# A six-stage decoder kernel: loading the first cross-attention unit inside the stage before, moving the query projections, and splitting the normed rows up front

## The chip, the core and the metric

The kernel runs on one core of a Trainium2 chip. TensorE (PE) multiplies matrices, VectorE (DVE), ScalarE (ACT) and GpSimd (POOL) do the elementwise work, SyncE (SP) issues most of the DMAs. The engines run their own instruction queues and meet at semaphores. The metric is the device time of one execution in microseconds (us), as the median of several runs.

## The reference

Two decoder layers over x, 4 sequences (b) of 256 tokens by 256 features; each sublayer is added to the residual. In sequence:

```
x = x + slot_attention(layernorm(x))            # layer 0, 16 heads, 64 slots a head
x = x + cross_attention(layernorm(x), ctx)      # layer 0, ctx: 4 x 1601 rows of 256
x = x + mixture_of_experts(layernorm(x))
x = x + differential_attention(layernorm(x))    # layer 1
x = x + masked_cross_attention(layernorm(x), ctx)
x = x + ternary_ffn(layernorm(x))

# the cross attention (16 heads of 16), the part that the change touches
q = rms_norm(x @ q_w + q_b) * norm_q_w
k = rms_norm(ctx_txt @ k_w + k_b) * norm_k_w;   v = ctx_txt @ v_w + v_b     # 1344 keys
ki = rms_norm(ctx_img @ k_img_w + ...) ;        vi = ctx_img @ v_img_w + ...  # 257 keys
out = (softmax(q k / 4) v + softmax(q ki / 4) vi) @ o_w + o_b
```

## The kernel before

Each sublayer is a stage with a list of steps. A step is a tuple such as ("q", 3), and each engine's program walks the same list in the same order and emits its own part of each step (SP the DMAs). Between two stages all five engines drain and meet (`boundary`). What runs on an engine is therefore ordered by the list alone, and every engine is in order.

The slot attention ("gsa") goes through 16 units (4 head groups x 4 sequences), unit m of which is spread over passes m to m+3. Before the first pass, `norm_steps(0, 0)` normalises and transposes the first sequence's 256 rows, and then the other six 128-row tiles follow. `h_split` b cuts the turned rows `hT` of sequence b into a high and a low part (`h_parts`): a cast on ACT (L748), a subtraction on POOL (L920). TensorE's products of queries and keys (`qk`, L1755 to L1757) read both parts of the sequence. In the kernel before, the split of sequence m+1 stands in pass m, woven between that pass's other steps.

Passes 12 to 18 also carry steps of the cross attention ("xa", `xa_early`): its weights, the key and value projections of sequence 0, its keys normed, turned, split into three bf16 parts (`xa_keys`) and stored to DRAM (`k_store`, L1109), and the queries of sequences 0 to 2. `queries(b)` is the set of six steps for one sequence: two tiles projected (L1464) and biased (L1560), one norm (`q_norm`, a chain of small DVE operations), two tiles turned (L1469) and split (L1362, L1367, L1369, L1374), one store to DRAM (L1105).

The cross attention stage has 16 units, 4 heads of one sequence each, of 13 key tiles ("steps" below: step m is the m-th key tile, unit n begins at step 13n). For unit n, `load` fetches keys and queries from DRAM into one of four buffers `kst`/`qst`: six key DMAs (L1100), six query DMAs (L1090), and for the first four loads one of constant rows (L987). `max` (32 matmuls L1137, each reduced on DVE, L1250) finds the largest score of each query; the negated maxima are turned and written into `qst` by six small DMAs (`neg_turn`, L1121). Then `exp` (L1156, ACT L1211) and `pv` (L1177) run over the 13 tiles. Meanwhile `projections(b)` and `xa_keys(b)` make the next sequence's keys in the steps 1 to 21 after the sequence before began. `xa_steps` gives each step a number and sorts by it: loads 0 to 3 stand ahead of everything, `queries(3)` at 4 to 10, the step `later` (weights for what follows, and about 3 MB copied into `moe_places_h`, L1679 and L1682) at 13, `max` of unit n from 13n-18.2 to 13n-5.2, `neg_turn` at 13n-3.2. A rotating set of three PSUM banks serves max, q, q_turn, kv and k_turn alike.

## Time and profile before

| what | value |
| --- | --- |
| median of 3 runs | 2068.56 us (2068.51 to 2073.98) |
| the profiled execution: its own time, its span | 2059.21 us, 2057.4 us |
| granted TensorE clock, mean over the span | 0.925 of full |
| PE, DVE busy, share of the span | 86%, 66% |
| ACT, POOL busy | 41%, 23% |
| slot attention stage, about | 0 to 653 us |
| cross attention stage, about | 653 to 1190 us |

Busy shares are averages over six stages with different limits, so they bound nothing by themselves. The table of windows gives for any stretch the busy time of each engine, the granted clock, and the share of the DMA engines that was busy. The timeline gives single instructions; the brackets at a row's end give the engine's idle time before it and what ended it.

### The profile page before, as it was taken

How to read it: one execution, taken by the hardware profiler on the slowest of the kernel's cores; microseconds unless marked ns; L12 is line 12 of the kernel's file. 1: busy time of each engine (PE TensorE's matmuls, PEld its weight loads, DVE VectorE, ACT ScalarE, POOL GpSimd, SP SyncE). 2: the span in 40 equal slices, each digit the busy share in tenths (PEclk: the TensorE clock that was granted, in tenths of full speed). 3: DMA queues.
4: the chain of work that ended last, by engine and by line, in shares of the span. 5: the costliest groups of instructions: out<-in, count | busy, mean ns of one | idle time of the engine just before them, and what ended most of it. 6: DMA issues, size and time to landing. Idle time of an engine off the chain costs nothing.

```text
span 2057.4 us, 32234 instructions
## 1 busy us (share of the span) xinstructions
PE 1769.9 (86%) x12150; PEld 1108.5 (54%) x12150; DVE 1348.0 (66%) x3123; ACT 838.1 (41%) x1339; POOL 465.6 (23%) x694
## 2 busy tenths in 40 slices
PE   4899999998963788989989979995887698999978
PEld 4788888888652233434434445663454244444446
DVE  6676676766575677687778543445455787888843
ACT  2333333333331145456455722441232165656651
POOL 4443444444122011020010021442000013211100
PEclk9999999999986699999999979998898699999988
DMA  3000010010014548228163064545320156655000
GB/s 113 5 27 11 21 32 11 24 61 1 16 40 113 94 93 144 32 91 101 34 118 45 2 229 162 203 167 114 73 61 20 39 73 127 76 89 80 7 1 21
DMA packets 91396, 142.65 MB, mean 69 GB/s; under 512 B 14549, under 2 KB 59737, under 8 KB 91242
## 3 DMA queue, kind: packets, MB, share of 16 engines
q1 hardware_dynamic: 78978, 118.87, 27.7%
q10 hardware_dynamic: 10392, 16.58, 2.8%
q0 software_dynamic: 1872, 5.13, 0.7%
q8 instruction: 98, 1.61, 0.3%
q14 instruction: 56, 0.46, 0.1%
HBM read 109.62 MB, written 32.03 MB: 69 GB/s over the span
## 4 chain that ended last, share of the span: by engine, by line
PE 63%; DVE 20%; issue 6%; ACT 4%; DMA 4%; SPq 2%; POOL 2%; ACTq 0%; POOLq 0%; DVEq 0%
PE bank L1177 8%; PE bank L1137 8%; PE bank L1156 7%; PE bank L1859 5%; PE bank L1478 4%; PE bank L1755 3%; PE bank L729 3%; PE bank L1878 3%; PE bank L1757 3%; PE bank L1756 3%; DVE xa_part_max L1250 2%; PE bank L2267 2%; SPq L1121 1%; DMA xa_qst<-xa_q_parts 1%; PE bank L2252 1%
## 5 line engine op out<-in xcount | busy, mean ns | idle before, releaser
L1250 DVE TENSOR_REDUCE xa_part_max<-bank 128x1 f32<-128x448 f32 (+1 forms) x512 | 273.5, 569 | 67.5 <-PE bank L1137 62.4
L1211 ACT ACTIVATE xa_e<-bank 128x1024 f32<-128x1024 f32 (+1 forms) x208 | 212.7, 1023 | 137.9 <-PE bank L1156 136.0
L1211 ACT ACTIVATE ca_e<-bank 128x1024 f32<-128x1024 f32 (+2 forms) x208 | 196.6, 957 | 99.3 <-PE bank L1156 91.9
L1250 DVE TENSOR_REDUCE ca_part_max<-bank 128x1 f32<-128x400 f32 (+1 forms) x384 | 205.8, 570 | 35.3 <-PE bank L1137 31.5
L1137 PE MATMUL bank<-xa_kst,xa_qst 122*128 122x448 bf16 (+1 forms) x512 | 171.4, 360 | 41.6 <-DMA xa_qst<-xa_q_parts 20.0
L1137 PE MATMUL bank<-ca_kst,ca_qst 125*128 125x400 bf16 (+2 forms) x512 | 160.8, 350 | 24.3 <-DMA ca_qst<-ca_q_parts 11.8
L1156 PE MATMUL bank<-xa_qst,xa_kst 128*128 128x256 bf16 (+1 forms) x832 | 128.6, 277 | 19.5 <-DMA xa_qst<-xa_negT 19.5
L1177 PE MATMUL bank<-xa_e,xa_vaug 128*17 128x256 f32 (+2 forms) x1792 | 140.7, 389 | 1.0 <-ACT xa_e L1211 0.6
L1177 PE MATMUL bank<-ca_e,ca_vaug 128*17 128x256 f32 (+2 forms) x1664 | 125.8, 375 | 7.9 <-ACT ca_e L1211 7.0
L1137 PEld LDWEIGHTS bank<-xa_kst,xa_qst 122*128 122x128 bf16 x512 | 48.7, 98 | 151.9 <-DVE xa_part_max L1250 85.0
L1156 PE MATMUL bank<-ca_qst,ca_kst 128*128 128x256 bf16 (+2 forms) x832 | 121.6, 269 | 0.3 <-ACT ca_e L1211 0.2
L933 POOL TENSOR_TENSOR gsa_qk<-gsa_qk,gsa_rot 128x512 f32<-128x512 f32 x64 | 81.9, 1280 | 169.5 <-DVE gsa_rot L849 169.5
L1137 PEld LDWEIGHTS bank<-ca_kst,ca_qst 125*128 125x128 bf16 x512 | 47.5, 98 | 121.7 <-DVE ca_part_max L1250 56.9
L1156 PEld LDWEIGHTS bank<-xa_qst,xa_kst 128*128 128x128 bf16 (+1 forms) x832 | 81.2, 100 | 54.3 <-DMA xa_qst<-xa_negT 22.9
L1478 PE MATMUL bank<-xa_wkv,shared 128*128 128x512 f32 (+2 forms) x224 | 108.3, 609 | 0.4
L1156 PEld LDWEIGHTS bank<-ca_qst,ca_kst 128*128 128x128 bf16 (+1 forms) x832 | 79.7, 101 | 27.3 <-issue 6.8
L1859 PE MATMUL bank<-moe_gu,moe_rowsT 128*128 x184 | 86.5, 593 | 0.1
L2373 DVE TENSOR_REDUCE da_neg<-bank 128x2 f32<-128x512 f32 x64 | 41.3, 687 | 51.8 <-PE bank L2267 51.8
L1322 POOL TENSOR_SCALAR_AFFINE_SELECT ca_e<-ca_e 128x248 f32<-128x248 f32 (+2 forms) x48 | 23.7, 507 | 223.2 <-ACT ca_e L1211 223.2
L847 DVE TENSOR_TENSOR gsa_qk<-bank,gsa_cos 128x512 f32<-128x512 f32 x64 | 43.6, 682 | 45.7 <-PE bank L1757 45.4
L1247 DVE CUSTOM_DVE_ANT_0 ca_masked_scores<-bank,ca_pen 128x272 f32<-128x272 f32 (+1 forms) x128 | 64.5, 504 | 10.9 <-PE bank L1137 10.0
L344 PE MATMUL bank<-ident,h 128*128 128x128 f32 x48 | 18.7, 390 | 58.6 <-DVE h L333 58.1
(373 smaller groups left out, 3994.6 us busy)
## 6 DMA issues: line engine op xcount, KB each, us to landing
xa_kst<-xa_k_parts SPq DMA_DIRECT2D x96, 200.1 KB, 8.7
ca_kst<-ca_k_parts SPq DMA_DIRECT2D x96, 200.1 KB, 7.4
xa_k_parts<-xa_parts SPq DMA_DIRECT2D x8, 1200.8 KB, 6.5
ca_k_parts<-moe_ctx_parts SPq DMA_DIRECT2D x8, 1200.8 KB, 5.7
moe_gu<-in_expert_gate_up SPq DMA_DIRECT2D x8, 1024.0 KB, 15.3
shared<-in_ctxT_split ACTq DMA_DIRECT2D x4, 1601.0 KB, 6.6
moe_ctxT<-in_ctxT SPq DMA_DIRECT2D x8, 800.5 KB, 8.1
ca_cv<-in_ctx ACTq DMA_DIRECT2D x4, 1536.0 KB
```

Source lines behind the costliest of these rows:

```text
L729: m = e.matmul(ps[:, 0:D], ogT[i][:, h_, :], wo[g % 2][:, h_, :], start=(h_ == 0), stop=(h_ == G4 - 1))
L933: e.tensor_tensor(qb[:], qb[:], rb[:], ALU.add).then_inc(*qk_ready(n))
L1137: e.matmul(work[:, 0:hi - lo], qb[0:self.AUG, h_, i * P:(i + 1) * P], kb[0:self.AUG, h_, lo:hi], start=True, stop=True).then_inc(*mx_mm(t, ...
L1156: mm = e.matmul(o, kb[:, j, k0:k0 + rows], qb[:, j, first:T], start=True, stop=True)
L1177: mm = e.matmul(bank[4][32 * j:32 * j + VW, s * T + lo:(s + 1) * T], vb[r0:r1, v, g * UNIT + j, :], self.e[m % 3][r0:r1, j, lo:T], start=f ...
L1211: e.activation(self.e[m % 3][0:rows, :, first:T], banks[m % 2][0:rows].rearrange("p a (h t) -> p (a h) t", t=T)[:, :, first:T], ACT.Exp, s ...
L1247: e.tensor_tensor_reduce(self.masked_scores[:, 0:hi - lo], work[:, 0:hi - lo], self.pen[:, i, 0:hi - lo], 1.0, FAR, ALU.add, ALU.max, top) ...
L1250: e.tensor_reduce(top, work[:, 0:hi - lo], AX.X, ALU.max).then_inc(*reduced(t, *step))
L1478: m = e.matmul(ps[r0:r1, :], xctx[:, c, k0 + r0:k0 + r1], wkv[s][:, c, :], start=(c == 0), stop=(c == DC - 1))
L1755: e.matmul(ps, l[:, 0], r[:, 0], start=(n == 0), stop=False)
L1756: e.matmul(ps, l[:, 0], r[:, 1], start=False, stop=False)
L1859: m = e.matmul(bank[j], l, r, start=(c == 0), stop=(c == DC - 1))
```

## The change

Five things. `h_split` of sequences 1 to 3 leaves the passes: each sequence is split as soon as its two tiles are turned, before the first pass (`normed_rows`). `queries(1)` and `queries(2)` leave the last pass of the slot attention. `load 0` joins pass 17, behind the store of the keys of sequence 0; for that its query buffer `qst0` is allocated among the early tiles, and SP waits for the slot attention's last `a` and `v` products first. In the cross attention `queries(b)` for b = 1, 2, 3 now stand at 10.5 to 21 steps after sequence b-1 began, beside `xa_keys(b)`. Loads 1, 2 and 3 stand at -99, 2 and 15 instead of ahead of everything.

```diff
@@ gsa_steps
+            def normed_rows(b):
+                for i in range(b * TB, (b + 1) * TB):
+                    yield "norm", 0, i
+                    yield "norm_turn", 0, i
+                yield "h_split", b
...
@@ ahead(m)
-                if m + 1 < B:
-                    yield "h_split", m + 1
@@ xa_early(m)
                     yield from xa_keys(0)
-                if m == GSA_UNITS + 2:
-                    yield from queries(1)
-                    yield from queries(2)
+                    yield "load", 0
@@ before the passes
-            for b in range(1, B):
-                for i in range(b * TB, (b + 1) * TB):
-                    yield "norm", 0, i
-                    yield "norm_turn", 0, i
+            yield from normed_rows(1)
+            yield from normed_rows(2)
+            yield from normed_rows(3)
@@ Attention
-                self.qst = [sb(f"qst{i}", [P, UNIT, T], BF16) for i in range(AHEAD)]
+                self.qst = [*qst, *(sb(f"qst{i}", [P, UNIT, T], BF16) for i in range(len(qst), AHEAD))]
@@ xa_steps
-            parts = [list(XA.flow()), spread(queries(B - 1), 4, 10), [(whole_unit, ("later", 0))]]
+            parts = [list(XA.flow()), *(spread(queries(b), (b - 1) * UNITS * whole_unit + 10.5, (b - 1) * UNITS * whole_unit + 21) for b in range(1, B)), [(whole_unit, ("later", 0))]]
...
-                if n % UNITS or not n:
-                    parts.append([(start - 3 * whole_unit + 1 if n >= AHEAD else n - 100, ("load", n))])
+                if n % UNITS:
+                    parts.append([(start - 3 * whole_unit + 1 if n >= AHEAD else -99 if n == 1 else start - 2 * whole_unit + 2, ("load", n))])
@@ xa_sp_step
+            elif kind == "load":
+                if n == 0:
+                    q.wait_ge(a_mm, G4 * GSA_UNITS - 1)
+                    q.wait_ge(v_mm, GSA_UNITS - 1, TB - 1)
+                if n < AHEAD:
+                    XA.stacks.constants_rows(q, n)
+                XA.load_sp(q, n)
```

SP at the end of the slot attention, in the kernel before: the store of the keys of sequence 0, two query stores (six DMAs), and after the boundary load 0, load 1 and the start of load 2.

```order
L1109 DMA xa_k_parts<-xa_parts 128x3x1601 x2
L1105 DMA xa_q_parts<-xa_q_split 128x2x256 x6
L987 DMA xa_kst<-in_consts 32x4x1601
L1100 DMA xa_kst<-xa_k_parts 16x4x1601 x6
L1090 DMA xa_qst0<-xa_q_parts 16x4x256 x6
L987 DMA xa_kst<-in_consts 32x4x1601
L1100 DMA xa_kst<-xa_k_parts 16x4x1601 x6
L1090 DMA xa_qst1<-xa_q_parts 16x4x256 x6
L987 DMA xa_kst<-in_consts 32x4x1601
```

The same place in the changed kernel (its line numbers are 1 to 9 higher).

```order
L1110 DMA xa_k_parts<-xa_parts 128x3x1601 x2
L988 DMA xa_kst<-in_consts 32x4x1601
L1101 DMA xa_kst<-xa_k_parts 16x4x1601 x6
L1091 DMA xa_qst0<-xa_q_parts 16x4x256 x6
L988 DMA xa_kst<-in_consts 32x4x1601
L1101 DMA xa_kst<-xa_k_parts 16x4x1601 x6
L1091 DMA xa_qst1<-xa_q_parts 16x4x256 x6
L1122 DMA xa_qst0<-xa_negT0 1x4x256 x6
L988 DMA xa_kst<-in_consts 32x4x1601
```

The two query stores have left this place, load 0 follows the key store directly, and the six small DMAs of unit 0's maxima come ahead of load 2; the boundary now stands between load 0 and load 1.

Further on in SP's queue, the kernel before: the end of load 3, the maxima of units 0 and 1 with the query store of sequence 3 between them, then the rows of `later`.

```order
L987 DMA xa_kst<-in_consts 32x4x1601
L1100 DMA xa_kst<-xa_k_parts 16x4x1601 x6
L1090 DMA xa_qst3<-xa_q_parts 16x4x256 x6
L1121 DMA xa_qst0<-xa_negT0 1x4x256 x6
L1105 DMA xa_q_parts<-xa_q_split 128x2x256 x3
L1121 DMA xa_qst1<-xa_negT1 1x4x256 x6
L1676 DMA xa_wo<-in_xa_o_w 128x2x256
```

The changed kernel, from the maxima of unit 1 to load 3.

```order
L1122 DMA xa_qst1<-xa_negT1 1x4x256 x6
L1685 DMA xa_wo<-in_xa_o_w 128x2x256
L1686 DMA xa_bo<-in_xa_o_b 128x256
L1687 DMA moe_wgate<-in_gate_w 128x2x8
L1688 DMA moe_places_h<-in_unsent 2944x2
L1691 DMA moe_places_h<-in_x 1024x256 x2
L1691 DMA moe_places_h<-in_x 896x256
L988 DMA xa_kst<-in_consts 32x4x1601
L1101 DMA xa_kst<-xa_k_parts 16x4x1601 x6
L1091 DMA xa_qst3<-xa_q_parts 16x4x256 x6
```

Load 3 has moved from the head of the stage to behind the copies into `moe_places_h`.

POOL at the start of the slot attention, before: splits of sequence 0 and of two weights, then the rotated queries and keys (`gsa_qk`), with the split of sequence 1 behind the fourth of them.

```order
L920 TENSOR_TENSOR gsa_h_parts<-hT,gsa_h_parts 128x2x256
L925 TENSOR_TENSOR gsa_wq<-gsa_w,gsa_wq 128x1024
L925 TENSOR_TENSOR gsa_wk<-gsa_w,gsa_wk 128x1024
L933 TENSOR_TENSOR gsa_qk<-gsa_qk,gsa_rot 128x512 x3
L906 AFFINE_SELECT gsa_aT<-gsa_aT 128x2x128
L933 TENSOR_TENSOR gsa_qk<-gsa_qk,gsa_rot 128x512
L920 TENSOR_TENSOR gsa_h_parts<-hT,gsa_h_parts 128x2x256
```

The same place in the changed kernel.

```order
L921 TENSOR_TENSOR gsa_h_parts<-hT,gsa_h_parts 128x2x256
L926 TENSOR_TENSOR gsa_wq<-gsa_w,gsa_wq 128x1024
L926 TENSOR_TENSOR gsa_wk<-gsa_w,gsa_wk 128x1024
L921 TENSOR_TENSOR gsa_h_parts<-hT,gsa_h_parts 128x2x256 x3
L934 TENSOR_TENSOR gsa_qk<-gsa_qk,gsa_rot 128x512 x3
L907 AFFINE_SELECT gsa_aT<-gsa_aT 128x2x128
L934 TENSOR_TENSOR gsa_qk<-gsa_qk,gsa_rot 128x512
```

The splits of sequences 1 to 3 stand ahead of the first `gsa_qk`.

## Rows read from the trace of the kernel before

**Rows 1.** Windows: us, engines busy (instructions), PE clock, DMA share, GB/s.
```profile
652.90:667.70 14.80, 0.00 (x0) 0.01 (x1) 2.42 (x5) 0.00 (x0) 3.04 (x1) 0.50 1.03 179
667.70:690.50 22.80, 20.51 (x47) 4.68 (x47) 22.02 (x47) 0.36 (x1) 0.84 (x4) 0.50 1.07 174
699.50:751.00 51.50, 47.99 (x222) 20.20 (x223) 30.92 (x88) 19.17 (x44) 2.13 (x6) 0.93 0.10 33
```

**Rows 2.** Timeline, 640 to 700 us: start, length, engine, line, operation, [idle before].
```profile
667.72 16.71 PE L1137 MATMUL bank<-xa_kst,xa_qst 122*128 122x448 bf16 x35 [17.97 <-DMA xa_qst<-xa_q_parts]
699.49 0.82 PE L1156 MATMUL bank<-xa_qst,xa_kst 128*128 128x256 bf16 x3 [9.56 <-DMA xa_qst<-xa_negT]
```

**Rows 3.** Timeline of the slot attention's last pass.
```profile
627.89 2.04 POOL L949 TENSOR_TENSOR gsa_og<-gsa_og,gsa_rr 128x512 f32<-128x512 f32 x2 [2.52 <-DVE gsa_rr L889]
633.25 1.06 PE L721 MATMUL bank<-ident,gsa_og 128*128 128x128 f32 x4
...
640.44 0.74 DVE L322 BATCH_NORM_STATS2 stats<-x 128x6 f32<-128x256 f32 x2
644.10 0.40 DVE L333 TENSOR_SCALAR h<-x,mv,rstd 128x256 f32<-128x256 f32 x1
650.77 0.67 POOL L1374 TENSOR_TENSOR xa_q_split<-xa_r,xa_q_split 128x256 bf16<-128x256 f32 x1 [0.23 <-DVE xa_q_split L1369]
```

**Rows 4.** Timeline of SP's DMA issues, 594 to 700 us.
```profile
625.40 1.63 SPq L1109 DMA_DIRECT2D xa_k_parts<-xa_parts  x2
...
653.12 0.35 SPq L987 DMA_DIRECT2D xa_kst<-in_consts  x1
...
686.71 3.79 SPq L1121 DMA_DIRECT2D xa_qst<-xa_negT  x6
```

**Rows 5.** Landing times of the key store issued at 625.40.
```profile
DMA to landing us min/median/max: 5.0/6.4/7.7
```

**Rows 6.** Timeline: unit 3's maxima, SP's issue and the matmul that waited.
```profile
808.79 3.66 SPq L1121 DMA_DIRECT2D xa_qst<-xa_negT  x6
...
814.39 0.61 PE L1156 MATMUL bank<-xa_qst,xa_kst 128*128 128x256 bf16 x4 [0.76 <-DMA xa_qst<-xa_negT]
```

**Rows 7.** Waits of PE, 22 to 150 us, and timeline around the first.
```profile
PE bank L1755 <- POOL gsa_h_parts L920: 9.6, 2, 5.6
...
42.23 0.55 PE L1755 MATMUL bank<-gsa_h_parts,gsa_wq 128*128 128x256 f32 x1 [5.65 <-POOL gsa_h_parts L920]
...
34.21 3.36 DVE L837 RECIPROCAL gsa_enz<-bank 128x512 f32<-128x512 f32 x1
...
34.88 0.63 ACT L748 CAST gsa_h_parts<-hT 128x512 fp32r<-128x512 f32 x1
```

**Rows 8.** One query set: windows of tiles xa_qq and xa_q_split, then timeline.
```profile
715.00:748.00 33.00, 0.82 (x4) 0.45 (x4) 1.73 (x4) 1.02 (x4) 1.00 0.07 17
...
715.00:748.00 33.00, 1.44 (x4) 0.73 (x2) 1.34 (x2) 1.00 0.07 17
...
717.27 1.03 PE L1464 MATMUL bank<-xa_wq,hT 128*128 128x256 f32 x4
...
729.60 0.16 DVE L1563 TENSOR_SCALAR xa_q_sv<-xa_q_ss 128x2 f32<-128x2 f32 x1
...
731.96 0.88 DVE L1568 SCALAR_TENSOR_TENSOR xa_qq<-xa_qq,xa_q_sr,xa_nq 128x256 f32<-128x256 f32 x2
```

**Rows 9.** Windows while the keys of sequences 1 and 2 are turned.
```profile
751.00:791.00 40.00, 32.57 (x267) 14.17 (x265) 35.04 (x82) 20.66 (x30) 9.84 (x18) 0.98 0.72 159
883.00:912.00 29.00, 23.47 (x188) 10.49 (x185) 27.00 (x65) 15.26 (x25) 8.31 (x13) 1.00 0.03 11
```

**Rows 10.** SP's copy in `later`, a window behind it, unit 3's first maximum on PE.
```profile
753.30 8.66 SPq L1682 DMA_DIRECT2D moe_places_h<-in_x  x3
...
775.00:780.00 5.00, 3.90 (x33) 1.72 (x32) 4.69 (x13) 2.72 (x5) 2.05 (x4) 1.00 0.01 2
...
779.85 0.36 PE L1137 MATMUL bank<-xa_kst,xa_qst 122*128 122x448 bf16 x1
```

More of the change, by code:

```diff
@@ L362, in build @@
         XA_TILES = TXT // P + 1 + 2
-        XA_EARLY = ("q", "q_norm", "q_turn", "q_store", "fetch", "kv", "k_norm", "k_scale", "k_turn", "k_store", "xa_w", "xa_const")
+        XA_EARLY = ("q", "q_norm", "q_turn", "q_store", "fetch", "kv", "k_norm", "k_scale", "k_turn", "k_store", "xa_w", "xa_const", "load")
         q_mm, q_biased, q_squared, q_scaled, q_ss_taken = local("gsa", "xa_q_mm"), local("gsa", "xa_q_biased"), local("gsa", "xa_q_squared"), local("gsa", "xa_q_scaled"), local("gsa", "xa_q_ss_taken")
@@ L992, in build, with __init__ @@
         class Attention:
-            def __init__(self, ctx, tag, keys, scale, tiles, chunks, sets, masked=False, k_dram=None, q_dram=None, stacks=None, vaug=(), parts=None):
+            def __init__(self, ctx, tag, keys, scale, tiles, chunks, sets, masked=False, k_dram=None, q_dram=None, stacks=None, vaug=(), parts=None, qst=()):
                 self.tag, self.keys, self.scale, self.tiles, self.chunks = tag, keys, scale, tiles, chunks
@@ L1406, in build @@
         qq, q_parts = sb("qq", [P, TB, D]), sb("q_split", [P, 3, DC, T], BF16)
-        XA = Attention(xa_ctx, "xa", CTX, HD ** -0.5, xa_tiles, [(0, third), (third, 2 * third), (2 * third, TXT), (TXT, CTX)], 2, vaug=(xa_vaug0,), parts=xa_parts)
+        xa_qst0 = sb("qst0", [P, UNIT, T], BF16)
+        XA = Attention(xa_ctx, "xa", CTX, HD ** -0.5, xa_tiles, [(0, third), (third, 2 * third), (2 * third, TXT), (TXT, CTX)], 2, vaug=(xa_vaug0,), parts=xa_parts, qst=(xa_qst0,))
         XA.x_stage = 2
@@ L1683, in xa_sp @@
                 else:
-                    if step[0] == "load" and step[1] < AHEAD:
-                        XA.stacks.constants_rows(q, step[1])
                     XA.sp(q, step)
```

## The prediction

> **What bounds the kernel now.** I read the page's busy shares first: TensorE leads with 86% of the span, so what it stands idle for is what there is to gain. The table of windows shows the largest hole, between the first two stages. From 652.9 to 667.7 us no TensorE work runs at all while the DMA engines are full (share 1.03); for 22.8 us more DVE is saturated (22.02 busy) by unit 0's maxima, with TensorE at half clock (0.50); only at 699.49 does the first score matmul start [rows 1, 2]. The timeline says what ended each wait: unit 0's query and key rows from DRAM at 667.72, and its six rows of maxima at 699.49, after 9.56 us in which TensorE had nothing [rows 2]. The first unit then is bound by TensorE, 47.99 of 51.5 us [rows 1]. Two other places matter: the start, where TensorE waits 9.6 us in two waits for POOL's split of a later sequence [rows 7], and the stretches in which keys are turned and split, where DVE is busy 35.04 of 40 and 27.00 of 29 us [rows 9].
>
> **The splits up front.** The first wait lasts 5.65 us, up to 42.23, so TensorE was free at 36.58 [rows 7]. What is late next is its PSUM bank, held until DVE's reciprocal ends at 34.21 + 3.36 = 37.57: 4.66 us can go. Of the second wait (9.6 - 5.6 = 4.0 us) I know no next bound, so 0 to 4.0 goes. Against it: each split's cast costs ACT 0.63 us between the copies that free the transposes' banks [rows 7], three of them 1.9 us, partly covered by DVE's norm of the next tile; I take 0.5. POOL's three subtractions fall where it has no queued work yet. Bounds: -8.7 + 0.5 at best, nothing gained (+1.9) at worst, if later passes were waiting for something else anyway. I take -6, near the two waits, since TensorE is the busy engine of the rest of that stage.
>
> **The hand-over.** Three things are in line: when load 0 lands, when unit 0's maxima are ready, when their six rows land.
> Load 0. It can go once the key store of sequence 0 is in DRAM: issued from 625.40, landing up to 7.7 us after [rows 4, 5], so about 633.1. Before, from the first issue at 653.12 to the first max at 667.72 it took 14.6 us [rows 2, 4]. The same 14.6 from 633.1 gives 647.7; the constant rows (of 1.8 MB a load, 0.4) go out while SP waits for the key store, which saves up to 0.7 of it. I take 647.0.
> Is the stage over by then? Before, POOL had both scaled tiles by 627.89 + 2.04 = 629.93, but TensorE's second turn of them started at 633.25, since a query turn in front of it waited for its norm chain: 3.3 us lost [rows 3]. Then came the output products, one more tile projection, the norm from its statistics at 640.44 to the first row tile at 644.10, and the last query split, which ran to 651.44 [rows 3]. Without the queries the statistics start 3.3 us and one 1.03 us projection earlier, at about 636, the first row tile is there 3.7 us later at 639.7, transposes and copies take some 2 us by my estimate from such tiles, so the boundary is at about 641.5 and, with DVE's memsets (2.42 us [rows 1]), a first max possible at 644. Load 0 at 647.0 is the later one. Gain so far 667.72 - 647.0 = 20.7.
> The maxima themselves stay 32 matmuls and reductions at DVE's pace; nothing changes there.
> The six small DMAs were issued from 686.71 to 690.50 and the matmul started at 699.49, 9.0 us after the last, behind loads 1 to 3 (the four loads went out from 653.1 with the DMA engines full, and these rows behind them landed at 699.5: some 44 us of transfers, 11 a load). Where the queue was less full, the same six ended at 812.45 and the matmul ran at 814.39: 1.9 us [rows 6]. In the change only load 1 is ahead of them; it goes out from 641.5 and both loads together need 22 us from 633, so the queue is empty by about 656, and the small DMAs go out at about 666. Gain 7.0. Together 27.7: the first score matmul at 671.8 on before's time axis. Bounds: 20.7 - 3 + 0 if load 0 shares its engines with load 1 and the small DMAs stay slow, 23.7 + 7.0 if the boundary alone decides.
> Load 2 is due at step 7.8, some 30 us after that, and goes out at once: hidden.
>
> **The query sets in the cross attention.** One set costs DVE 1.73 us on `xa_qq`, 1.44 on its split and 731.96 - 729.60 = 2.36 for the norm chain: 5.5 us. It costs TensorE 0.82 for turns and 2 x 1.03 for projections: 2.9 us [rows 8]. Before, one set (sequence 3) lay in unit 0, where TensorE bounds: -2.9. Now three sets lie where keys are turned, and there DVE is 88 and 93% busy [rows 9]: 3 x 5.5 = +16.5. Lower bound: TensorE's share alone or DVE's leftover idle, about 2.5 a set, +7.6. Upper bound: a set's length when nothing hides it, from the 640.44 that its last projection just preceded to the last split at 651.44 [rows 3], 11.0 a set, +33.0. I take DVE's busy time, because the rows show DVE as the engine without slack there.
>
> **Load 3 behind `later`.** The 3 MB copy of `later` went out from 753.30, and the DMA engines were idle again (share 0.01) from 775 [rows 10]: about 22 us of transfers. Unit 3's first max was at 779.85 [rows 10]. All of this moves up by 27.7 + 2.9 = 30.6, the max only by 25.1 (a query set now lies before it): due at 754.8. The copies end at 744.4 and load 3's 11 us end at 755.4, 757 with landing. TensorE would stand some 2 us: +2 (0 to 8).
> The Trainium skill (DMA: Bandwidth & Descriptors, Queues, rings and completion order) says that each DMA engine consumes descriptors in ring order, which speaks against this place for the load. By that rule the +2 stands, since load 3 cannot overtake the copies; if the engines took turns between them instead, load 3 would land before it is due and the sum would be 2 us better. No row of before has a load behind these copies.
>
> **Sum.** -6 - 27.7 - 2.9 + 16.5 + 2 = -18.1 us. The profiled execution took 2059.21, so it would take 2041.1. The timed runs have a median 9.35 higher; the saving lies in waits and counts the same there: 2068.56 - 18.1 = 2050.5. I count 0.3%, 6.2 us, as the least that a measurement tells from no change.
>
> **Rivals.**
> A, no change: each set costs its unhidden 11.0 us, since TensorE, in order and with three banks for everything, stops at the turn until the norm chain is through. For it: exactly this happened at 633.25 [rows 3]. Against: in the stage's steps the turns are spaced some 1.75 steps apart, with scores and maxima between. Sum: -6 - 27.7 - 2.9 + 33.0 + 2 = -1.6, 2067.0. 10%.
> B, slower: the clock does not come back. After the hand-over TensorE starts unit 0 from half clock (0.50) and got 0.93 over the 51.5 us [rows 1]. Should it stay at 1.2 GHz through the unit, its 47.99 us would be 47.99 x 0.93 / 0.50 = 89, +41 us, and the result 2050.5 + 41 = 2091.5. It decides from the point where the lost 18.1 is made up: 44.6 us of full-speed work in 44.6 / (48 + 18.1), a granted clock under 0.68 in that unit. Against: a longer hole before ended with the full clock. 4%. The Trainium skill (TensorE: Matmul & The Clock Gate, Seeing it yourself) notes a clock seen stuck low for 50 us and more; this case's trace shows no such thing in busy work after the hand-over.
> C, the early load does not do what it says: it still competes with load 1 or waits at its semaphores, and only the shorter tail counts. The first max is then 14.6 us behind the boundary of 641.5, at 656.1: gain 11.6 in place of 20.7, sum -9.0, 2059.6. For it: in before's full queue a load took the full 14.6. Against: 8 us lie between the key store's landing and the boundary. 9%.
> D, the sets are nearly free: 7.6 in place of 16.5, because reductions slide into the units behind, where DVE has room. Sum -27.0, 2041.6. 14%.
> The forecast, 2050.5, own range 2043 to 2058: 63%.
>
> **Range and chances.** 2039 to 2066 reaches from a little below D to just short of A and holds C; outside are A, B and a start and hand-over both at their best. Faster by over 0.3% (below 2062.4): 62 of the forecast's 63, 13 of D, 6 of C, 0.81. Within 0.3%: 1 + 3 + 6 of A, 1 of D, 0.11. Slower: B, 4 of A, 0.08.
>
> **What the profile after would show.** The first max of unit 0 at about 641 and its first score matmul at about 666 on the new axis (647.0 and 671.8, 6 us earlier from the start); the idle time before that matmul under 4 us, not 9.56. The two POOL waits at the start gone. No query rows between the slot attention's last output products and the boundary. The windows in which keys are turned 4 to 7 us longer each, with DVE above 90%. A wait of a few us for DMA at unit 3's first max. Wrong if the first max comes later than 650, if a key window grows by more than 9 us, or if TensorE waits over 8 us at load 3.

## The result and the profile after

| kernel | median, us | runs, us |
| --- | --- | --- |
| before | 2068.53 | 4 runs, 2064.72 to 2073.98 |
| changed | 2046.15 | 4 runs, 2042.23 to 2050.22 |

The ratio is 0.989, with a 95% interval of 0.9856 to 0.9924: the change saves 22 us, more than the 6.2 that a measurement can tell. The profiled execution took 2042.23 us (before 2059.21). Its page begins so:

```profile
span 2040.4 us, 32227 instructions
...
PE 1770.0 (87%) x12150; PEld 1102.9 (54%) x12150; DVE 1350.8 (66%) x3123; ACT 837.3 (41%) x1339; POOL 464.0 (23%) x694
```

The shares have hardly moved, so the saving must be looked for in places. First the hand-over. The timeline of PE in the changed kernel, the same two matmuls as in [rows 2], and the first maximum of unit 3 as third:

```profile
632.03 16.72 PE L1138 MATMUL bank<-xa_kst,xa_qst 122*128 122x448 bf16 x35 [5.93 <-DMA xa_qst<-xa_q_parts]
656.33 1.04 PE L1157 MATMUL bank<-xa_qst,xa_kst 128*128 128x256 bf16 x4 [2.08 <-DMA xa_qst<-xa_negT]
739.67 0.35 PE L1138 MATMUL bank<-xa_kst,xa_qst 122*128 122x448 bf16 x1 [0.24 <-DMA xa_qst<-xa_q_parts]
```

The waits of 17.97 and 9.56 us are now 5.93 and 2.08. SP's issues say why (start, length, line):

```profile
609.12 0.89 SPq L1110 DMA_DIRECT2D xa_k_parts<-xa_parts  x2
610.11 1.01 SPq L988 DMA_DIRECT2D xa_kst<-in_consts  x1
617.74 2.72 SPq L1101 DMA_DIRECT2D xa_kst<-xa_k_parts  x6
620.51 2.77 SPq L1091 DMA_DIRECT2D xa_qst<-xa_q_parts  x6
626.57 0.32 SPq L988 DMA_DIRECT2D xa_kst<-in_consts  x1
...
651.03 4.20 SPq L1122 DMA_DIRECT2D xa_qst<-xa_negT  x6
...
704.64 8.36 SPq L1691 DMA_DIRECT2D moe_places_h<-in_x  x3
713.04 4.31 SPq L988 DMA_DIRECT2D xa_kst<-in_consts  x1
```

SP issues the keys of load 0 at 617.74, 8.6 us after the key store (609.12), when the store has landed; its landing times, which answer to [rows 5]:

```profile
DMA to landing us min/median/max: 4.6/6.4/8.2
```

The last query row of load 0 lands at 631.84 and TensorE takes it at 632.03: 14.3 us from the issue of its keys, against 14.6 from its first issue before. The six small rows (651.03 to 655.23) have only load 1, issued from 626.57 and landed by 644.59, ahead of them, and the matmul starts 1.1 us behind the last; before it was 9.0 us. The end of the slot attention, which answers to [rows 3]:

```profile
613.43 2.17 PE L722 MATMUL bank<-ident,gsa_og 128*128 128x128 f32 x8 [5.88 <-POOL gsa_og L950]
...
621.43 0.74 DVE L322 BATCH_NORM_STATS2 stats<-x 128x6 f32<-128x256 f32 x2
624.87 0.74 DVE L333 TENSOR_SCALAR h<-x,mv,rstd 128x256 f32<-128x256 f32 x2
```

TensorE's eight turns of the scaled tiles follow POOL in one run, no query work comes behind, and the boundary is at 626.6.

Windows answering to [rows 1]: the empty stretch, the maxima, and the first unit from its first score matmul:

```profile
626.60:632.00 5.40, 0.00 (x0) 0.00 (x0) 2.42 (x5) 0.00 (x0) 3.04 (x1) 0.50 1.09 164
632.00:651.00 19.00, 17.39 (x40) 4.04 (x40) 18.30 (x39) 0.36 (x1) 0.84 (x4) 0.50 0.58 69
656.30:707.80 51.50, 49.43 (x243) 21.07 (x244) 29.24 (x75) 19.25 (x42) 0.83 (x4) 0.93 0.39 77
```

5.4 us are left of the 14.8 without TensorE. Unit 0 had the same granted clock as before, 0.93.

At the start, the waits of PE from 22 to 150 us, which had 9.6 us for POOL's splits [rows 7]:

```profile
PE bank L641 <- ACT gsa_es L759: 2.2, 3, 1.6
PE bank L714 <- POOL gsa_w2T L907: 1.9, 1, 1.9
PE bank L1762 <- DVE gsa_rot L850: 1.8, 2, 1.3
...
PE bank L1762 <- DVE gsa_enz L838: 1.0, 1, 1.0
```

TensorE's waits for POOL's splits are gone (the columns are us in total, times, longest). In the stretches in which the keys of the next sequence are made, I take the same 8, 16 and 16 steps of both kernels, from the start of one exponential on ACT (L1211, L1212 after) to that of another: steps 12 to 20, 60 to 76, 112 to 128. Before:

```profile
754.57:779.09 24.52, 19.14 (x147) 8.78 (x146) 23.28 (x58) 12.87 (x22) 7.64 (x12) 1.00 0.80 126
875.16:917.68 42.52, 35.09 (x283) 15.75 (x281) 39.07 (x99) 23.16 (x38) 10.68 (x22) 1.00 0.20 73
1006.95:1049.77 42.82, 35.08 (x283) 15.73 (x281) 39.09 (x99) 23.16 (x38) 10.69 (x22) 1.00 0.20 72
```

After:

```profile
707.51:738.64 31.13, 22.71 (x155) 10.74 (x153) 28.49 (x77) 14.00 (x26) 8.93 (x14) 0.89 1.05 167
836.78:886.80 50.02, 39.29 (x295) 18.58 (x293) 44.46 (x119) 24.79 (x44) 11.97 (x24) 0.93 0.20 71
974.83:1024.92 50.09, 39.53 (x295) 18.39 (x293) 44.49 (x119) 24.74 (x44) 11.98 (x24) 0.93 0.20 72
```

They grew by 6.6, 7.5 and 7.3 us, while DVE's busy time grew by 5.2, 5.4 and 5.4. The granted clock, 1.00 before, fell in each of them, and TensorE has three waits of one kind in the stage, 11.1 us together, that took 1.0 us before, this one in the first window:

```profile
719.19 1.12 PE L1186 MATMUL bank<-ident,xa_accs 128*128 128x128 f32 x4 [3.70 <-DVE xa_part_max L1251]
```

### The profile page after: what moved, and what is told of

It reads as the page before. It is cut to its first block, busy times and chain, and to the rows that moved or that the text cites. A ratio compares the mean times of both kernels' runs of the same rounds, so it can differ in the third digit from the quotient of the medians.

```text
span 2040.4 us, 32227 instructions
## 1 busy us (share of the span) xinstructions
PE 1770.0 (87%) x12150; PEld 1102.9 (54%) x12150; DVE 1350.8 (66%) x3123; ACT 837.3 (41%) x1339; POOL 464.0 (23%) x694
## 4 chain that ended last, share of the span: by engine, by line
PE 62%; DVE 20%; issue 5%; DMA 4%; ACT 4%; SPq 2%; POOL 1%; ACTq 0%; another core or an unknown queue 0%; POOLq 0%; DVEq 0%
PE bank L1178 8%; PE bank L1138 8%; PE bank L1157 7%; PE bank L1866 5%; PE bank L1480 5%; PE bank L1762 3%; PE bank L730 3%; PE bank L1885 3%; PE bank L1764 2%; PE bank L1763 2%; DVE xa_part_max L1251 2%; PE bank L2274 2%; DMA xa_qst<-xa_q_parts 2%; PE bank L2259 1%; DMA xa_k_parts<-xa_parts 1%
## 5 line engine op out<-in xcount | busy, mean ns | idle before, releaser
L1212 ACT ACTIVATE xa_e<-bank 128x1024 f32<-128x1024 f32 (+1 forms) x208 | 212.4, 1021 | 119.7 <-PE bank L1157 118.0
L1212 ACT ACTIVATE ca_e<-bank 128x1024 f32<-128x1024 f32 (+2 forms) x208 | 196.4, 956 | 101.9 <-PE bank L1157 93.9
L1157 PEld LDWEIGHTS bank<-xa_qst,xa_kst 128*128 128x128 bf16 (+1 forms) x832 | 81.7, 101 | 47.4 <-DMA xa_qst<-xa_negT 14.3
L1157 PEld LDWEIGHTS bank<-ca_qst,ca_kst 128*128 128x128 bf16 (+1 forms) x832 | 80.0, 102 | 27.8 <-issue 7.3
L1248 DVE CUSTOM_DVE_ANT_0 ca_masked_scores<-bank,ca_pen 128x272 f32<-128x272 f32 (+1 forms) x128 | 64.6, 504 | 11.7 <-PE bank L1138 11.0
L1178 PEld LDWEIGHTS bank<-xa_e,xa_vaug 128*17 128x17 f32 (+2 forms) x1792 | 29.7, 95 | 73.0 <-issue 56.1
```

The source lines that it names most:

```text
L1157: mm = e.matmul(o, kb[:, j, k0:k0 + rows], qb[:, j, first:T], start=True, stop=True)
L1178: mm = e.matmul(bank[4][32 * j:32 * j + VW, s * T + lo:(s + 1) * T], vb[r0:r1, v, g * UNIT + j, :], self.e[m % 3][r0:r1, j, lo:T], start=f ...
L1212: e.activation(self.e[m % 3][0:rows, :, first:T], banks[m % 2][0:rows].rearrange("p a (h t) -> p (a h) t", t=T)[:, :, first:T], ACT.Exp, s ...
L1248: e.tensor_tensor_reduce(self.masked_scores[:, 0:hi - lo], work[:, 0:hi - lo], self.pen[:, i, 0:hi - lo], 1.0, FAR, ALU.add, ALU.max, top) ...
```

## The experiments

A common measure is the start of the same instruction against the kernel before: the last copy of turned exponentials in the slot attention (`gsa_esT<-bank` on ACT, 529.91 us in the kernel before, so some 120 us ahead of that stage's end; "start"), the first exponential of the cross attention (step 0), later ones by step, and the last. Eleven kernels ran beside the one before, each profiled once, the changed one and `best` twice; us against before, whose profiled execution is the reference throughout:

| kernel | start | step 0 | 28 | 60 | 128 | last | median (ratio to before) |
| --- | --- | --- | --- | --- | --- | --- | --- |
| changed | -14.1 | -43.2 | -40.4 | -38.4 | -24.8 | -24.2 | 2046.15 (0.989) |
| after_again | -9.9 | -38.0 | -35.1 | -29.7 | -11.7 | -10.2 | 2048.05 (0.9885) |
| split_only | -9.8 | -8.4 | -10.7 | -11.2 | -7.6 | -5.9 | 2059.23 (0.9926) |
| no_split | -0.2 | -28.2 | -25.2 | -23.4 | -4.5 | -2.1 | 2058.10 (0.9918) |
| loads_front | -9.9 | -24.9 | -24.8 | -23.7 | -7.6 | -6.9 | 2058.65 (0.9938) |
| load_only | -4.7 | -25.1 | -19.5 | -20.6 | -16.9 | -11.7 | 2050.49 (0.9911) |
| q_only | -4.9 | -12.2 | -12.5 | -10.0 | +6.6 | +9.9 | 2081.64 (1.0073) |
| q_beside_kv | -9.3 | -37.3 | -27.8 | -21.3 | -17.1 | -14.7 | 2047.35 (0.9864) |
| q_kv_load3 | -9.2 | -37.7 | -36.7 | -30.5 | -26.1 | -26.8 | 2041.68 (0.9882) |
| load3_first | -10.8 | -39.1 | -35.8 | -31.5 | -12.6 | -11.0 | 2048.55 (0.9889) |
| rows_first | -15.2 | -46.9 | -44.7 | -41.7 | -26.2 | -25.5 | 2041.87 (0.9872) |
| best | -12.2 | -43.1 | -42.1 | -35.8 | -29.1 | -28.3 | 2032.35 (0.9841) |
| best_again | -6.7 | -38.9 | -37.9 | -31.4 | -25.1 | -24.2 | 2035.24 (0.9831) |

The first row is the result above. The other medians come from three groups of runs on one chip each, with the kernel before at 2072.94 (split_only, no_split, loads_front, q_beside_kv), 2065.88 (load_only, q_only, q_kv_load3, best) and 2072.86 (after_again, which is the changed kernel once more, load3_first, rows_first, best_again). Between groups only ratios compare. The profiled execution of before (2059.21) is itself faster than all its timed runs, so a profile's own time against it understates a gain. The column "start" also shows how far single profiles can be trusted: no_split, load_only and q_only run the same steps as before up to there, and read -0.2, -4.7 and -4.9.

**Split alone.** The kernel before, with `("h_split", b)` behind each sequence's turned tiles and out of the passes, as in the change.

```diff
+            def normed_rows(b):
...
+                yield "h_split", b
...
-                if m + 1 < B:
-                    yield "h_split", m + 1
```

> The kernel before with one part of the change: the rows of sequences 1 to 3 are split as soon as they are turned, ahead of the first pass. Theory W (waits and clock): the two waits of 9.6 us go, and with them the half-clock stretches that followed them in the trace of before (50.2 to 57.0 and 63.8 to 67.2 us); the slot attention ends 11 to 15 us earlier, the whole kernel by about as much. Theory P (the prediction's term): 6 us. Rival C: the 16 us that the changed kernel was ahead at its key store came from the query sets taken out of the tail or from chance; then this part alone gives 0 to 3 us.

Measured: ratio 0.9926 (0.9902 to 0.995), 14 us by the medians, as theory W had it for the whole kernel. The kernel is 13.6 us ahead at the seventh `gsa_aT` tile (75.35 us before) and 9.8 at "start". All ten profiles of kernels with the splits up front lie 10.7 to 13.8 us ahead at that early tile, the four others (before included) 0 to 1.6; at "start" the ten lie 6.7 to 15.2 ahead, 10.7 on average, the four 2.5 on average. So the splits are worth some 12 us early and some 8 at "start", not 6; part is given back on the way. (The half-clock stretches that the expectation names are misplaced: 63.8 to 67.2 us had the full clock, 69.7 to 73.1 half of it. The rows stand further below.)

**All but the split.** The changed kernel with the split back in the passes.

```diff
             def scores(m):
...
+                if m + 1 < B:
+                    yield "h_split", m + 1
```

> The changed kernel with the row splits put back into the passes, all else as changed. Theory W: 11 to 15 us slower than the changed kernel, 8 to 11 us faster than before. Theory P: 6 us slower than the changed kernel. Rival C: as fast as the changed kernel within 3 us.

Measured: 0.9918 (0.9891 to 0.9944), 15 us by the medians, more than the 8 to 11 expected. The start does not move (-0.2), step 0 comes 28.2 us earlier: the hand-over alone is 28.0 us. By ratios the changed kernel (0.9885 to 0.989) is some 6 us ahead of this one, though in another group.

**All loads at the head of the stage.** The changed kernel with one expression back; load 0 stays early.

```diff
-                    parts.append([(start - 3 * whole_unit + 1 if n >= AHEAD else -99 if n == 1 else start - 2 * whole_unit + 2, ("load", n))])
+                    parts.append([(start - 3 * whole_unit + 1 if n >= AHEAD else n - 100, ("load", n))])
```

> The changed kernel with loads 2 and 3 back at the head of the cross attention, ahead of unit 0's maxima in SP's queue. Theory Q (the small rows of maxima queue behind the loads' data): the first score matmul waits 6 to 9 us for its rows in place of 2.08, and the kernel is 4 to 7 us slower than the changed one. Rival L (the six rows are simply slow at that place, whatever is ahead): the wait stays at about 2 us and the time is unchanged. The wait for load 3 (0.24 us) goes in both.

Measured: 0.9938 (0.9916 to 0.9959). Here the six small rows stand behind loads 1 to 3, as before. PE's first score matmul, and SP's issue of the rows it waited for:

```profile
674.59 1.03 PE L1157 MATMUL bank<-xa_qst,xa_kst 128*128 128x256 bf16 x4 [15.37 <-DMA xa_qst<-xa_negT]
...
656.00 3.79 SPq L1122 DMA_DIRECT2D xa_qst<-xa_negT  x6
```

In the changed kernel's second profile, which has the same start, they were issued at 656.15. Here load 3's last query row, issued at 652.34, landed at 673.77, and the matmul followed 0.8 us later: the small rows came only when everything issued ahead of them was in. TensorE waited 15.37 us for them, not 2.08, which is more than the 6 to 9 expected. From the start to step 0 this kernel gains 15.0 us, the changed one in an execution with the same start 28.1: without the late place of loads 2 and 3, 13 us of the early load's worth are lost again.

**Loads alone.** The kernel before with load 0 early and loads 1 to 3 placed as in the change; the query sets stay where they were.

```diff
                     yield from xa_keys(0)
+                    yield "load", 0
...
-                    parts.append([(start - 3 * whole_unit + 1 if n >= AHEAD else n - 100, ("load", n))])
+                    parts.append([(start - 3 * whole_unit + 1 if n >= AHEAD else -99 if n == 1 else start - 2 * whole_unit + 2, ("load", n))])
```

> The kernel before with only the loads moved: load 0 in pass 17 of the slot attention, loads 1, 2, 3 at -99, 2 and 15; the query sets stay in the last pass and in unit 0, the row splits in the passes. Theory H (the hand-over ends at the later of boundary and load 0; the small rows land 2 us after their issue if only load 1 is ahead): the boundary stays at about 653, so the first max starts at about 655.5 (12 us earlier), the first score matmul at about 680 (19 us earlier), and load 3 is then awaited for 6 to 9 us behind the copies, since no query set stands before unit 3's maxima. Net 10 to 14 us faster than before. Rival R (the early load brings nothing without the shorter tail): 0 to 4 us.

Measured: 0.9911 (0.989 to 0.9933), 15 us by the medians, a little more than the 10 to 14 expected. Step 0 against the start: -20.4, with a tail that is as long as before. The first unit-3 maximum, however, waits for load 3:

```profile
760.85 0.53 PE L1138 MATMUL bank<-xa_kst,xa_qst 122*128 122x448 bf16 x1 [5.95 <-DMA xa_qst<-xa_q_parts]
```

**Query sets alone.** The kernel before, with only the query sets moved.

```diff
-                if m == GSA_UNITS + 2:
-                    yield from queries(1)
-                    yield from queries(2)
...
-            parts = [list(XA.flow()), spread(queries(B - 1), 4, 10), [(whole_unit, ("later", 0))]]
+            parts = [list(XA.flow()), *(spread(queries(b), (b - 1) * UNITS * whole_unit + 10.5, (b - 1) * UNITS * whole_unit + 21) for b in range(1, B)), [(whole_unit, ("later", 0))]]
```

> The kernel before with only the query sets moved to 10.5 to 21 steps after the sequence before began; loads and row splits as before. Theory H: the boundary comes 11 us earlier, load 0 still takes its 14.6 us behind it, the small rows still 9 us; unit 0 is 4 us shorter; three sets cost 7.3 us each: 11 + 4 - 22 = 7 us slower than before. Rival P (a set costs its DVE busy time of 5.5 us): 1 to 2 us slower. Rival S (sets are nearly free): 7 us faster or more.

Measured: 1.0073 (1.0055 to 1.009), slower by 16 us by the medians, not by 7. The shorter tail gives only 7.3 us at step 0, since the small rows, issued sooner after the same four loads, wait longer:

```profile
651.46 16.72 PE L1134 MATMUL bank<-xa_kst,xa_qst 122*128 122x448 bf16 x35 [16.23 <-DMA xa_qst<-xa_q_parts]
687.30 1.04 PE L1153 MATMUL bank<-xa_qst,xa_kst 128*128 128x256 bf16 x4 [13.62 <-DMA xa_qst<-xa_negT]
```

From step 12 to 128 the three sets and what follows them then cost 24.9 us. By itself this part of the change is a loss. Beside the early load it is no gain either: load_only (loads alone, 0.9911) and no_split (loads and sets, 0.9918) are equal within their intervals. The shorter tail gives 7.6 us more at the hand-over (28.0 against 20.4), and the sets in their new place take it back: from the start to the last exponential no_split gains 1.9 us and load_only 7.0. So where the change puts them, moving the sets was not needed for its result. No run has the splits and the loads without the sets; the product of the two ratios (0.9926 and 0.9911) would put it at 0.984 by estimate.

**The sets beside the keys' projections.** A set now lies in the first unit of a sequence, where TensorE bounds, not where keys are turned.

```diff
-  spread(queries(b), (b - 1) * UNITS * whole_unit + 10.5, (b - 1) * UNITS * whole_unit + 21)
+  spread(queries(b), (b - 1) * UNITS * whole_unit + 2, (b - 1) * UNITS * whole_unit + 10)
```

> The changed kernel with each query set at 2 to 10 steps after the sequence before began, beside the key and value projections, where TensorE is the busy engine and DVE has room, in place of 10.5 to 21, beside the turning of keys, where DVE is full. Theory D (a set costs what the busy engine of its place pays): each set costs 3 to 4 us instead of the 7.3 us read from the two traces, and the kernel is 9 to 12 us faster than the changed one. Rival S (a set costs its DVE time wherever it stands, since reductions are displaced into the next stretch): within 3 us of the changed kernel.

Measured: 0.9864 (0.9827 to 0.99). That is within the interval of the changed kernel, so the 9 to 12 us expected did not come. The sets are cheaper, though. Sets 2 and 3 add 4.7 us each, in steps 52 to 60 and 104 to 112 (the whole of unit 4, steps 52 to 64, is 4.7 longer), and steps 60 to 76 and 112 to 128 cost next to nothing. Set 1 lies in unit 0, which carried a set before too; there steps 0 to 12 took 57.25 us, before 54.01, at a lower clock (0.89 against 0.93). But the wait for load 3 is there:

```profile
752.65 0.53 PE L1138 MATMUL bank<-xa_kst,xa_qst 122*128 122x448 bf16 x1 [6.07 <-DMA xa_qst<-xa_q_parts]
```

The last copy into `moe_places_h` landed at 741.49, the first piece of load 3 at 743.21 and its last at 752.41. So the 0.24 us of the changed kernel are not a fast transfer but a covered one: the set ahead of that maximum holds it back, steps 12 to 20 being 6.6 us longer.

**The same with load 3 ahead of the copies.**

```diff
-  [(whole_unit, ("later", 0))]
+  [(whole_unit + 2.5, ("later", 0))]
```

> The kernel with the query sets beside the key and value projections (2 to 10), and the step `later` moved from 13 to 15.5, behind load 3 in SP's queue. Theory Q: the 6.07 us that TensorE waited for load 3 in that kernel go, 5 to 7 us faster than it and 9 to 12 us faster than the changed kernel. Rival C (the copies of `later` only collide with the next transfers, the key store and load 4, and the wait turns up there): no faster than with the query sets moved alone.

Measured: 0.9882 (0.9864 to 0.9899). In this profile the wait at unit 3 is gone (load 3, issued from 712.72, landed by 727.81, ahead of the copies) and steps 0 to 28 lose 1.0 us in all, against 9.5 in q_beside_kv. Steps 0 to 12 are 0.2 us longer than before, which also had a set there, and 3.1 longer than in the changed kernel's second profile, which has none: that is set 1's price. The windows of steps 52 to 60 here, and before:

```profile
800.91:844.66 43.75, 41.53 (x198) 18.58 (x197) 29.72 (x91) 15.92 (x40) 3.17 (x5) 1.00 0.24 31
836.14:875.16 39.02, 38.88 (x186) 16.66 (x185) 25.18 (x71) 14.38 (x33) 1.84 (x3) 1.00 0.28 35
```

TensorE is busy for 95% of the first and over 99% of the second, and 2.65 of the 4.73 us between them are its own busy time. The ratio does not show the 5 to 7 us expected over q_beside_kv, nor the 9 to 12 over the changed kernel: all three kernels lie within each other's intervals.

**The last edit alone.** The changed kernel with `whole_unit + 2.5` only.

> The changed kernel with only the 3 MB copy of the next stage 2.5 steps later, so that load 3 is issued ahead of it. Theory G (load 3 is covered by the query set in unit 2, TensorE waited only 0.24 us there): no gain, 2047 us, the wait at unit 3's first maximum at 0. Rival H (the prediction's 2 us at that place): 2 us faster, 2045 us. If the later copy is itself missed by the masked stage, 1 to 3 us slower.

Measured: 0.9889 (0.9866 to 0.9912), 2048.55 beside 2048.05 for the changed kernel in the same group: no gain, as the cover says. The 2 us of the prediction are not there.

**Early rows of load 0.** The changed kernel, with constants and query rows of load 0 issued ahead of the wait for the key store.

```diff
+            elif kind == "load_rows":
+                q.wait_ge(a_mm, G4 * GSA_UNITS - 1)
+                q.wait_ge(v_mm, GSA_UNITS - 1, TB - 1)
+                XA.stacks.constants_rows(q, n)
+                XA.loaded_before = (n,)
+                XA.load_sp(q, n)
```

The keys follow at the old place (the other half is shown with the last kernels).

> The changed kernel with one thing more: the constant rows and the query rows of load 0 are issued ahead of the wait for the store of the keys, and only its keys behind it. Theory E (load 0 still sets the first maximum, since it came 4 us or more after the boundary): the first maximum of unit 0 comes 2 us earlier against the steps of the slot attention, 2044.5 us. Rival F (the boundary or the wait for load 1 ahead of the small rows sets it): no gain, 2047 us.

Measured: 0.9872 (0.9848 to 0.9896), 2041.87. The first maximum now waits for keys, for 3.51 us; in the changed kernel of the same group it was 6.82:

```profile
628.33 16.71 PE L1139 MATMUL bank<-xa_kst,xa_qst 122*128 122x448 bf16 x35 [3.51 <-DMA xa_kst<-xa_k_parts]
```

Start to step 0 gains 31.7 us, against 28.1. So load 0 was still the later of the two, by at least 3.3 us. The runs (2034.17 to 2050.29) overlap those of the changed kernel, so its 6 us in the median are not shown to be more than that.

**The changed kernel once more**, and **all three edits together** (beside the keys, load 3 first, early rows), in two groups.

```diff
-                if n < AHEAD:
-                    XA.stacks.constants_rows(q, n)
-                XA.load_sp(q, n)
+                    XA.keys_sp(q, n)
+                else:
+                    if n < AHEAD:
+                        XA.stacks.constants_rows(q, n)
+                    XA.load_sp(q, n)
```

That is the second half of the early rows; the other two edits are the lines shown above.

> The changed kernel itself, beside the others of this call and the kernel before on one chip. Expected: 2047 us, ratio to the kernel before 0.989. Theory 1 (the trace's account): first maximum 29 us plus the start's 10 to 14 earlier, three query sets some 7 us each. Theory 2 (the scatter between executions is as large as the parts): another execution differs in the start by several us, through half-clock stretches of 3.4 us.

> As the last, and in addition the constant rows and the query rows of load 0 are issued before the keys of sequence 0 are turned, so that only its six key DMAs wait for the key store. Theory K (the first max waits for the last DMA issued behind the key store's landing): 3 to 4 us come off the wait for load 0 (5.9 us in the changed kernel), until the boundary and DVE's memsets decide; 2 to 4 us faster than the last. Rival B (the DMA engines' throughput decides, not the issue): within 1 us of the last.

> The changed kernel with the query sets of a sequence beside its keys (steps 2 to 10 instead of 10.5 to 21), the 3 MB copy of the next stage 2.5 steps later, behind load 3, and the early rows of load 0. Theory 1: each part keeps what it gave when it was put in alone or last (sets beside the keys and load 3 ahead about 4 us at the end of the cross attention, early rows 2 us): 2037 to 2040 us, ratio to the changed kernel of the same call 0.995 to 0.997. Rival: the 12 us that separated the two kernels in separate calls are scatter between calls, and here they differ by less than 3 us.

Measured: the changed kernel 2048.05 (2041.02 to 2057.41), 0.9885 (0.986 to 0.991). All three edits: 2032.35, 0.9841 (0.9808 to 0.9873), and again 2035.24 (2031.98 to 2038.97), 0.9831 (0.9808 to 0.9854). In one group all five of its runs lie below all six of the changed kernel: a version 13 us faster than the changed one, 38 faster than before. That is more than the 7 to 10 us expected; `best` against q_kv_load3, which differs from it by the early rows alone, is 9 us faster in the medians where 2 to 4 were expected, with runs that overlap. Windows from the first score matmul of unit 0 on, its first unit and the rest of the stage, in the changed kernel's second profile:

```profile
661.50:713.00 51.50, 49.45 (x237) 20.31 (x238) 28.62 (x74) 19.08 (x41) 0.83 (x4) 0.91 0.41 76
713.00:1176.00 463.00, 408.70 (x3264) 183.60 (x3266) 341.71 (x820) 243.84 (x337) 52.24 (x122) 0.97 0.43 74
```

And in best_again:

```profile
660.60:712.00 51.40, 46.77 (x227) 20.04 (x227) 31.18 (x89) 19.26 (x45) 2.17 (x6) 0.96 0.36 76
712.00:1162.00 450.00, 407.75 (x3274) 182.10 (x3276) 337.21 (x804) 243.25 (x334) 50.93 (x120) 0.97 0.44 77
```

Together the two windows are 13.1 us shorter; TensorE's busy time fell by 3.6 of it (458.2 to 454.5), so most of what went is idle time.

## Why the prediction held, and where its sizes were off

The forecast was 2050.5 us against a median of 2046.15, inside its own range of 2043 to 2058. The largest term, the hand-over, was right in mechanism and size. That the sum came so close is partly luck: in both profiles the start gave more than forecast (8.1 and 3.9 us) and the sets cost more (4.9 and 3.6); the rest of the stage, put at nothing, cost 1.3 and 10.6. By its terms, in us:

| term | predicted | changed, first profile | second profile | by itself |
| --- | --- | --- | --- | --- |
| splits up front | -6 | -14.1 | -9.9 | -9.8 (split_only) |
| hand-over, start to step 0 | -27.7 | -29.1 | -28.1 | -28.0 (no_split) |
| one set less in unit 0, steps 0 to 12 | -2.9 | -3.9 | -2.9 | |
| three sets in key stretches | +16.5 | +21.4 | +20.1 | |
| load 3 | +2 | 0.2 | 0 | 0 (load3_first) |
| the rest of the stage | 0 | +1.3 | +10.6 | |
| end of the cross attention | -18.1 | -24.2 | -10.2 | |

**The hand-over was right, step by step.** With the start's 14.1 us added back, the boundary lies at 640.7 on before's axis (predicted 641.5), the first maximum at 646.1 (647.0) and the first score matmul at 670.4 (671.8). That the small rows wait behind whatever SP issued before them was the assumption on which the rest stood, and loads_front tests it: 15.37 us with three loads ahead, 2.08 with one. Its size there was underestimated: the prediction's lower bound, rows still slow after an early load, had 20.7 - 3 for the gain, and loads_front kept 15.0.

**The start was mis-sized.** The prediction took 6 us from the two waits of 9.6 [rows 7]. They went entirely. In their place came 1.0 us for DVE's reciprocal (`gsa_enz`), just what the prediction's bound for the first wait left (5.65 - 4.66), and 1.9 us for POOL's `gsa_w2T` (0.2 before); all of TensorE's listed waits from 22 to 150 us fell from 16.7 to 9.2 us. Beyond the waits, the clock moved. Before, the 6.8 us that begin in the first wait ran at half the clock, and so did two shorter stretches later. Rows of before:

```profile
39.00:45.80 6.80, 3.57 (x17) 3.60 (x18) 1.05 (x2) 0.00 (x0) 6.20 (x5) 0.51 0.01 2
52.60:56.00 3.40, 2.78 (x7) 2.27 (x8) 0.00 (x0) 0.48 (x1) 0.45 (x1) 0.53 0.00 0
69.70:73.10 3.40, 3.40 (x18) 3.40 (x18) 0.69 (x1) 0.00 (x0) 0.87 (x1) 0.53 0.02 5
```

The first window in the changed kernel, at full clock, and its only low stretch up to 120 us:

```profile
39.00:45.80 6.80, 6.79 (x47) 5.66 (x45) 5.05 (x8) 0.85 (x2) 5.75 (x4) 1.00 0.14 30
86.70:90.10 3.40, 3.40 (x18) 2.95 (x17) 2.84 (x5) 0.36 (x1) 1.02 (x1) 0.53 0.68 215
```

With the waits went 6.8 us at 1.2 GHz in the same place. Over 39.0 to 45.8 us all four kernels with the splits in the passes were granted 0.50 to 0.57, and all ten profiles with the splits up front 1.00. TensorE was busy 9.75 us in the three rows of before; at full clock that is some 4.9 less, which with the 7.5 us of waits makes 12.4 by estimate, and 13.6 were measured at the seventh tile. So the step that was too small is "I take -6": it counted waits alone and priced nothing for the clock. Whether the waits themselves lowered the clock, or something else that the same edit moves, no run separates. What is given back between there and "start", and the spread there (6.7 to 15.2 us ahead), is open: kernels with the same steps up to that point differ by as much. Against the 6 forecast, "start" gives 14.1 in this profile, 9.9 in the second and some 8 as the difference of the averages.

**The sets were mis-sized in the step "I take DVE's busy time".** DVE's busy time grew by what was counted (16.0 over the three stretches, predicted 16.5), but the stretches grew by 21.4: DVE's own idle time rose by 5.4. The 3.70 us in which TensorE waited for a maximum at L1186, and the clock falling from 1.00 to 0.89 and 0.93, lie in the same windows; how the 5.4 us divide between the two is not shown. The sign to look for, DVE above 90%, held in the first window only: 92, 89 and 89%. That the place matters is shown by q_kv_load3 and the two runs of all edits. With the sets in the first units of a sequence, steps 0 to 128 are 11.6, 14.0 and 13.8 us longer than before, against 18.3 and 26.4 in the two profiles of the changed kernel; set by set it is 3.1, 4.7 and 4.7 us, where the changed kernel has 5.9 to 7.5 in each of its stretches. The 4 to 7 us a window of the prediction were passed by half a microsecond in both profiles. The prediction did not ask what the sets' move is worth beside an early load: load_only shows the change without it to be as fast as no_split with it.

**Load 3** was predicted within 3 us (due 754.8, there at 757; taken at 739.67, which is 753.8 on before's axis). The wait fell away since load 3's last row landed at 739.43, 3.5 us earlier than forecast on before's axis, and the set ahead of the maximum took 6.6 us, not 5.5. Both kernels without that set show a wait of 6 us, and with load 3 ahead of the copies it vanishes, so the transfer does stand behind the copies. The Trainium skill (DMA: Bandwidth & Descriptors, Queues, rings and completion order) says that each DMA engine consumes descriptors in ring order, the rule that the prediction weighed. The runs agree: in q_beside_kv load 3 began to land 1.7 us after the last copy, in q_kv_load3 it was in before they were.

**The rivals.** A (sets at 11 us each): no, 7.1. B (the clock stays low): no, 0.93 in unit 0, as before. C (the early load does not help): no; load_only gains 20.4 at the hand-over with a tail that is not shortened. D (sets nearly free): not here, though the median lies between it and the forecast; at steps 2 to 10 the three cost 12.5 us (3.1, 4.7 and 4.7), about half way between its 7.6 and the 16.5 of the forecast.

**Behind the cross attention** the first profile goes from -24.2 to -17.0 at the span's end, the second from -10.2 to -1.7, split_only from -5.9 to +7.0, best_again only from -24.2 to -23.9. Before's profiled execution lies below all its timed runs, so part of this may be the reference and not the change; by medians the saving is 22.4. How executions of one kernel come to differ by 14 us at the end of one stage is open.

## What to carry to other kernels

An early load keeps its worth only if the small transfers due next are not queued behind the bulk that follows: of 28.1 us at the hand-over, 15.0 were left with the other loads ahead. Move the first load forward and the others back, as one edit. Work taken off the tail of a stage must be cheaper in its new place than in the tail: it gave 7.6 us at the hand-over here, and three sets cost 20 to 21 us in the stretches where DVE was over 90% busy before, 12.5 in the units that TensorE bounds. Compare also with the kernel that leaves them where they were. A single profile of a kernel against another's can be off by 5 us and more at a place that the edit does not touch. A transfer that shows no wait may be covered by the very work you mean to move next, so look at what stands ahead of it before moving.

## What the runs showed of the hardware

Six small DMAs took 1.1 us from their last issue to the matmul with one load ahead of them, and 14.8 (659.79 to 674.59) behind three, 0.8 us after the last row of the third had landed. The granted clock over one stretch of 6.8 us (39.0 to 45.8) was 0.50 to 0.57 in four kernels in which TensorE had waited 5.6 us for a split there, and 1.00 in all ten profiles without that wait. Two profiled executions of the same kernel differed by 14 us at the end of one stage.
